# Four layers in one kernel: a running count as one scan, logits between the first expert products, constants and rounded weights in other places

## The reference

```
x = x + L0_xattn(layernorm(x), ctx);  x = x + L0_ffn(layernorm(x))
x = x + L1_xattn(...);                x = x + L1_ffn(...)   # 32 experts, 6 of 3 groups of 8, capacity 48, shared expert
x = x + L2_xattn(...);                x = x + L2_ffn(...)   # 8 experts, 2 a row, and a shared one
x = x + L3_xattn(...);                x = x + L3_ffn(...)   # 32 experts, 8 a row
```

```
# L3_ffn, t rows, 32 experts of width 96            # choice of the k largest, ties to the lower index
scores  = softmax(x @ wg.T)                         # weights, idx = top_k(scores, 8)
weights = weights / sum(weights)
out[t]  = sum over chosen e: weights[t, e] * ((silu(x @ w1[e]) * (x @ v1[e])) @ w2[e])

# L3_xattn, 16 batches of 128 rows, 16 query heads and 8 key heads of 128
xq      = fp8(bf16(clip(ln(x) / in_scale)))         # q, k, v from own rows, qx for the context
q, k    = ln(xq @ wq), ln(xq @ wk);  v = xq @ wv    # "own" pass
qx      = ln(xq @ wqx);  kx, vx = context @ w_kv_x  # "cross" pass
cat     = [softmax(q k) v, softmax(qx kx) vx]
out     = fp8(cat / smooth) @ wproj * scales
```

## Time and profile before

| | |
|---|---|
| time, median of 3 runs | 2699.9 us (2689.95 to 2700.28) |
| the profiled execution, its own time and span | 2686.2 us, 2683.2 us |
| mean granted TensorE clock | 0.923 |
| TensorE products / weight loads busy | 2252.8 us (84%) / 1647.3 us (61%) |
| VectorE, ScalarE, GpSimd busy | 1824.3 (68%), 1528.2 (57%), 1504.4 (56%) |
| layer 1's experts, 605 to 890: TensorE mostly busy | 264.1 of 295 us between 605 and 900 |
| layer 2's experts, 1110 to 1303 | TensorE 176.7 of 193 us |
| layer 3's attention, 1303 to 2236 | TensorE 850.2, VectorE 762.7, ScalarE 753.8 of 933 us |
| layer 3's experts, 2239.4 to 2683.2 | TensorE 420.7 of 444 us |

### The profile page before, as it was taken

How to read it: one execution, slowest core, us unless ns; L and a number is a source line. 1 busy time by engine, 2 the same in 40 slices (tenths; PEclk the granted TensorE clock), 3 DMA queues, 4 the chain that set the end, 5 groups by cost and what they waited for, 6 DMA issues and landing times. The chain is left out here.

```text
span 2683.2 us, 45578 instructions
## 1 busy us (share of the span) xinstructions
PE 2252.8 (84%) x14565; PEld 1647.3 (61%) x14574; DVE 1824.3 (68%) x3801; ACT 1528.2 (57%) x3413; POOL 1504.4 (56%) x1496
## 2 busy tenths in 40 slices
PE   4998243979899588699489999989999987999998
PEld 2333021537645343488367777768888876788886
DVE  3887485766446365455788888878888876566565
ACT  0777383763120166344488989878887873344443
POOL 5452103630001453386188888777888873888882
PEclk9999665898999799799799999999999998999999
DMA  5333101543040334234110000110000001433433
GB/s 131 81 91 78 56 0 61 164 131 133 4 187 8 81 82 101 69 120 125 47 33 0 0 0 0 36 38 24 4 6 4 2 1 42 116 112 113 119 111 84
DMA packets 120164, 174.19 MB, mean 65 GB/s; under 512 B 25549, under 2 KB 78957, under 8 KB 117183
## 3 DMA queue, kind: packets, MB, share of 16 engines
q1 hardware_dynamic: 119423, 171.57, 22.2%
q10 hardware_dynamic: 576, 0.52, 0.1%
HBM read 122.06 MB, written 11.48 MB: 50 GB/s over the span
## 5 line engine op out<-in xcount | busy, mean ns | idle before, releaser
L2993 POOL TENSOR_SCALAR a_raw<-a_raw,a_mu,a_dev 128x128 f32<-128x128 f32 x640 | 576.6, 913 | 10.2 <-issue 10.2
L527 DVE TENSOR_REDUCE a_mraw<-a_wave_ps 128x4 f32<-128x1024 f32 (+1 forms) x256 | 307.4, 1218 | 108.2 <-PE a_wave_ps L359 105.5
L415 ACT ACTIVATE a_et<-a_wave_ps 128x1024 f32<-128x1024 f32 x256 | 262.2, 1027 | 67.5 <-PE a_wave_ps L376 63.1
L2983 POOL TENSOR_TENSOR a_dev<-a_var,a_minus_half 128x24 f32<-128x24 f32 x32 | 135.0, 4217 | 163.1 <-DVE a_var L3351 163.1
L3189 ACT ACTIVATE a_weights<-a_sp_ps,a_nmax 128x128 f32<-128x128 f32 x512 | 184.2, 395 | 45.2 <-DVE a_nmax L3364 43.7
L1757 DVE TENSOR_TENSOR f3e_hidden_low<-f3e_hidden,f3e_hidden_high 128x512 fp32r<-128x512 f32 x96 | 117.9, 1228 | 126.1 <-ACT f3e_hidden_high L1710 125.7
L3105 PE MATMUL a_o_ps<-a_wparts,a_catq 128*128 128x256 bf16 x1536 | 188.8, 273 | 7.7 <-DVE a_catq L3385 7.6
L1618 POOL TENSOR_TENSOR f3e_product<-f3e_silu,f3e_up 128x512 f32<-128x512 f32 x96 | 143.4, 1496 | 71.5 <-PE f3e_u_ps L1637 43.5
L3022 PE MATMUL a_p_ps<-a_wkv,a_xq 128*128 128x512 f32 x640 | 179.1, 414 | 3.8 <-DVE a_wkv L3263 3.3
L393 PE MATMUL a_o_ps<-a_et,a_vt 128*32 128x256 f32 x2048 | 165.2, 395 | 17.0 <-ACT a_osb L445 15.3
L3022 PE MATMUL a_p_ps<-a_wq,a_xq 128*128 128x512 f32 x512 | 152.8, 429 | 26.9 <-ACT a_vv L3208 15.9
(11 more groups left out here) (440 smaller groups left out, 5779.3 us busy)
## 6 DMA issues: line engine op xcount, KB each, us to landing
f_w<-in_f_w SPq DMA_DIRECT2D x16, 1216.0 KB, 8.7
a_qs<-a_parts SPq DMA_DIRECT2D x144, 128.0 KB, 2.4
f_raw<-in_f_w SPq DMA_DIRECT2D x60, 256.0 KB, 3.2
a_ks<-a_parts SPq DMA_DIRECT2D x96, 128.0 KB, 2.4
f3e_spread<-f3e_shares SPq DMA_DIRECT2D x64, 192.0 KB, 3.0
f2e_spread<-f2e_shares SPq DMA_DIRECT2D x36, 256.0 KB, 3.3
f3e_spread<-f3e_shares SPq DMA_DIRECT2D x64, 128.0 KB, 3.1
f_raw<-in_f_w SPq DMA_DIRECT2D x60, 128.0 KB, 3.6
```

What stands on the lines that cost most here:

```text
L415: self.nc.scalar.activation(self.et[:, g % self.WAVES_HELD, :, :], self.wave_ps[:, self.second_place[g][0], :, :], ACT.Exp, scale=self.sca ...
L527: v.tensor_reduce(out, wave.rearrange("p u (c n) -> p u c n", n=N), AX.X, ALU.max).then_inc(self.max_taken, 1)
L2993: mm = nc.gpsimd.tensor_scalar(head, head, mu[:, parity(b), h:h + 1], dev[:, parity(b), h:h + 1], ALU.subtract, ALU.mult)
```

## The change

It has four parts.

**The running count as a scan.** `choose` makes the count with one `tensor_tensor_scan` over all rows' numbers in one line: each value is the one before times `go_on` plus `equal`. `go_on` is 1.0, and 0.0 at the first expert of each row, so that the count starts anew; `group_starts` makes it by two memsets, ahead of the router. In layer 1 the experts' and the groups' counts both go this way, and the work that stood between two steps of the old count (`between("counts")`) now comes behind the scan.

**Logits between the first gate products (layers 2 and 3).** `normalised_transposed` and `logits_and_parts` are no longer called. `run` takes their work: TensorE turns the rows in four blocks of 512, makes the logits the other way round (`make_logits`: the gate's columns are the weights, 512 rows the moving side, two products for each of four row blocks, which write to partitions 0, 32, 64 and 96), makes `gate_up(0)`, turns the logits back with four transposes (`turn_logits`), makes `gate_up(1)` and goes on. ScalarE copies the turned rows and makes the first two of the four `x_high` parts ahead of the logits, the last two behind the early evictions; `x_low` likewise, the last two behind the share copy on VectorE. SP loads the first weight tile, then the gate, then the others; GpSimd cuts the first weight tiles as they arrive. In layer 3 the choice is run inside `softmax_rows`, while ScalarE makes the exponential.

**Layer 1's constants.** `places`, `same`, `owner` and `place` are loaded at the end of SP's list in f1r, behind the experts' first six weight loads, and f1d and f1c only wait for them.

**Layer 3's attention.** The cross weights go through three raw buffers: the two halves of `wraw` and `spare`, which is the room of `exponent` and `magic`, free once the last rows are rounded (`xq_ready` of `B`). `load_cross` issues them. `next weights` has eight places: 0 to 5 in the step of batch B - 3, 6 and 7 in that of B - 2, so six tiles in the first of the two steps and two in the second, where it was four and four. `next output` 0 and 1 move to other places within their steps. The own output weights' second pair is cut inside the third step (`parts of output` and `left of output`) and not behind it. The rows of batch 1 are normalised before the low parts of the weights (`normalise_rows(1)` in `cut_weights`) and not in the task "rows" behind them. In the order lists the entries other than `next weights`, `next output` and the new two stand in the same order as before.

The core of the diff:

```diff
+def group_starts(nc, st, name, n):
+
+    go_on = st.sb(name + "_go_on", [P, B, n])
+    nc.vector.memset(go_on[:, :, :], 1.0)
+    nc.vector.drain()
+    nc.vector.memset(go_on[:, :, 0:1], 0.0)
+    nc.vector.drain()
+    return go_on
+
+
+def choose(nc, values, k, n, chosen, st, name, go_on, between=lambda place: None):
...
+    run = st.sb(name + "_run", [P, B, n])
...
     kth = over(top[:, :, k - 1], n)
+    v.tensor_tensor(equal[:, :, :], values[:, :, :], kth, ALU.is_equal)
     v.tensor_tensor(above[:, :, :], values[:, :, :], kth, ALU.is_gt)
-    v.tensor_tensor(equal[:, :, :], values[:, :, :], kth, ALU.is_equal)
     v.drain()
+    v.tensor_tensor_scan(run[:, :, :].rearrange("p b n -> p (b n)"), go_on[:, :, :].rearrange("p b n -> p (b n)"),
+                         equal[:, :, :].rearrange("p b n -> p (b n)"), 0.0, ALU.mult, ALU.add)
     v.tensor_reduce(count[:, :], above[:, :, :], AX.X, ALU.add)
-
-    src, step, turn = equal, 1, 0
-    while step < n:
-        dst = runs[turn]
-        v.tensor_tensor(dst[:, :, step:], src[:, :, step:], src[:, :, :n - step], ALU.add)
-        v.tensor_copy(dst[:, :, :step], src[:, :, :step])
-        if step == 4:
-            between("counts")
-        v.drain()
-        src, step, turn = dst, 2 * step, 1 - turn
+    between("counts")
+    v.drain()
     between("ranks")
-    v.tensor_tensor(chosen[:, :, :], src[:, :, :], over(count[:, :], n), ALU.add)
+    v.tensor_tensor(chosen[:, :, :], run[:, :, :], over(count[:, :], n), ALU.add)
...
+                    load_weights(0)
+                    sp.dma_start(gate_tile[:, :, :], gate_source).then_inc(gate_in, 16)
+                    for target, source in self.loads:
+                        sp.dma_start(target, source).then_inc(self.w_in, 16)
+                    m = 1
+                    for _ in range(self.RAW + 2 + self.early // 4):
                         load_weights(m)
                         m += 1
...
+                        pe.wait_ge(x_ready, 2 * h + j + 1)
...
+                    def turn_rows(tb):
+                        wait(pe, xs_taken, tb - 1)
+                        for u in range(4):
+                            pe.wait_ge(xs_ready, 4 * tb + u + 1)
+                            for c in range(2):
+                                last = nc.tensor.transpose(y_ps[:, tb % 2, c, u * P:u * P + P],
+                                                           xs[:, tb % 2, u, c * P:c * P + P], ident[:, :])
+                        last.then_inc(xs_turned, 1)
+
+                    def make_logits():
+                        pe.wait_ge(gate_in, 16)
+                        pe.wait_ge(xs_taken, 4)
+                        for c in range(2):
+                            for tb in range(4):
+                                last = nc.tensor.matmul(by_expert[32 * tb:32 * tb + E_GATE, :], gate_tile[:, c, :],
+                                                        xnt[:, c, tb * 512:tb * 512 + 512], start=(c == 0), stop=(c == 1))
+                        last.then_inc(logits_done, 1)
+
+                    def turn_logits():
+                        pe.wait_ge(logits_taken, 1)
+                        for k in range(4):
+                            last = nc.tensor.transpose(by_token[:, k * P:k * P + P], logits_kept[:, k * P:k * P + P],
+                                                       ident[:, :])
+                        last.then_inc(logits_turned, 1)
+
+                    for tb in range(4):
+                        turn_rows(tb)
+                    make_logits()
+                    gate_up(0)
+                    turn_logits()
+                    gate_up(1)
+                    for n in range(2, self.early):
...
+                    turned_rows(0)
+                    high_rows(0)
+                    turned_rows(1)
+                    high_rows(1)
+                    turned_rows(2)
+                    turned_rows(3)
+                    act.wait_ge(logits_done, 1)
+                    nc.scalar.copy(logits_kept, by_expert).then_inc(logits_taken, 1)
                     router_act(act)
                     for n in range(self.early):
                         evict(n)
+                    high_rows(2)
+                    high_rows(3)
...
+                    low_rows(0)
+                    low_rows(1)
+                    router_prepare()
+                    dve.wait_ge(logits_turned, 1)
+                    nc.vector.tensor_copy(logits[:, :, :].rearrange("p (t k) e -> p k t e", t=4),
+                                          by_token.rearrange("p (k t e) -> p k t e", k=4, t=4)[:, :, :, 0:E_GATE])
+                    nc.vector.drain()
                     router_dve(dve).then_inc(share_ready, 1)
                     dve.wait_ge(share_turned, B // 2)
                     nc.vector.tensor_copy(sharet[0:E, 0:T // 2], share_ps[:, 0:T // 2]).then_inc(low_copied, 1)
+                    low_rows(2)
+                    low_rows(3)
...
-            on_act, on_dve = softmax_rows(nc, block, logits, probs, E, rt, "sm")
+            on_act, on_dve = softmax_rows(nc, block, logits, probs, E, rt, "sm",
+                                           lambda dve: choose(nc, logits, K, E, chosen, rt, "ch", go_on[0]))
...
+                        sp.dma_start(places[:, :], dram["f1_places"]).then_inc(places_in, 16)
+                        sp.dma_start(same[:, :], dram["f1_same"]).then_inc(places_in, 16)
+                        sp.dma_start(owner[:, :, :].bitcast(I16), dram["f1_owner"]).then_inc(owner_in, 16)
+                        sp.dma_start(place[:, :], dram["f1_place"]).then_inc(owner_in, 16)
...
-        exponent = sb("exponent", [P, 4, 2, P], BF16)
-        magic = sb("magic", [P, 4, 2, P], BF16)
+        rounding = sb("rounding", [P, 2, 4, 2, P], BF16)
+        exponent, magic = rounding[:, 0, :, :, :], rounding[:, 1, :, :, :]
+
+        spare = rounding[:, :, :, :, :].rearrange("p e k c n -> p (e k c n)").bitcast(F32)
 
...
+                def load_cross(k):
+                    if k < 2:
+                        sp.wait_ge(out_ready, k + 3)
+                    elif k == 2:
+                        sp.wait_ge(xq_ready, B)
+                    elif k < 3 + TILES:
+                        sp.wait_ge(low_ready, TILES + k - 2)
+                    else:
+                        sp.wait_ge(out_ready, U + 1)
+                    if k < TILES:
+                        sp.dma_start(cross_staged(k), weight_piece(dram, TILES + k)).then_inc(cross_in[k % 3], 16)
+                    else:
+                        u = k - TILES
+                        sp.dma_start(out_staged(U + u), dram["a3_cross_wproj"][:, 4 * u:4 * u + 4, :]
+                                     ).then_inc(cross_in[k % 3], 16)
...
-                    if b == B - 3:
+                    if b == (B - 3 if j < 6 else B - 2):
                         if j == 0:
                             act.wait_ge(projected, L * (B - 1) + 4)
+                        if j == 4:
+                            act.wait_ge(projected, L * B)
+                        if j == 6:
+                            act.wait_ge(values_projected, M * B)
                         high_part(TILES + j)
-                    if b == B - 2:
-                        if j == 0:
-                            act.wait_ge(projected, L * B)
...
                 def cut_weights():
+                    normalise_rows(1)
                     for t in range(TILES):
                         low_part(t)
...
                 def rows_task(b, k):
-                    if not is_own(b):
-                        return
+                    if is_own(b) and not (isinstance(b, int) and b == 1):
+                        normalise_rows(b)
+
+                def normalise_rows(b):
```

235 lines of the change are left out of this document (107 added, 128 removed), and 12 rows, old and new, of tables (CROSS_ORDER, OWN_ORDER).

## The result

The changed kernel takes 2668.5 us (median of 5 runs, 2667.3 to 2673.5), the one before 2694.4 in the same comparison (5 runs, 2690.0 to 2700.3). The ratio is 0.9907, with a 95% interval of 0.9893 to 0.9921: 25 us faster, between 21 and 29. Its profiled execution has a span of 2665.4 us, where before's had 2683.2. That is only 17.8 less, because stages whose code is the same differ by some us from run to run. So each stage is measured here over several traces: of the old code there is a second trace, or a third, from the experiments that keep it, and of the changed code up to twelve, as each experiment touches few stages.

What follows compares the result with a forecast made beforehand. It took stage heads, waits for constants and layer 3's handover, not TensorE-bound loops, as the question. Terms 12.5 + 4.8 + 6.2 + 5.8 + 5.0 = 34.3 off 2686.2 gave 2651.9, 2665 in median terms; range 2646 to 2686.

Steps and rivals of the forecast that it cites:

- the handover: Layer 3's attention, four steps after the first batch: six-and-two weight tiles, third buffer, earlier output cuts gain 5.0 us.
- The worst case of the forecast: Handover: first step takes two more tiles at 2.4, second gives back only part; 3 us lost.
- the rival that had 0.18: Layer 3's attention: the handover gives its bound, 13 us and not 5, 8 more, so 2657; chance 0.18.
- layer 2's router: Layer 2's experts: router takes 8.5 us, less 0.9 for the count; in a stage term of 4.8 us.
- layer 3's experts: Largest term: new head, scan and no share wait start block 7 12.7 us earlier, 12.5 counted; bounds 9 and 14.
- The sentence on cover: Layer 3's experts: copies, DMA trips and short steps, 12.6 us, fit under five blocks, 13.7; failure costs 1 to 2.
- layer 1's constants: Layer 1's experts: loading constants in the router removes waits of 2.9 us (VectorE) and 3.3 (TensorE), together 6.2.
- the early rows: Layer 3's attention, start: second batch's rows made before the low parts, so statistics end 4.8 us earlier.
- The output pair cut inside the step: Layer 3's attention, start: cutting the second output-weight pair inside the step fills ScalarE waits, 1.0 us, between -1 and 2.
- The rival on the clock: Expert heads, layers 2 and 3: clock stays at 0.50 through early blocks, 20 us less gained, 2685; chance 0.10.
- The rival on late constants: Layer 1: constants come late behind six loads of 1.2 MB, 3 us lost, 2668; chance 0.04.
- the one on tile buffers: Layer 3's attention: tile buffers become the chain, making the kernel slower, 2714 or more; chance 0.03.

Runs made afterwards that it cites:

- the last experiment: Changed kernel with old handover places (three buffers kept), first silu and first cast early, four early blocks in layer 2: 2660.6 us, ratio 0.9862 to before.

## Why the prediction was right, and where it was not

The sign and the range held: 2668.5 in 2646 to 2686, and 0.88 had been put on faster. The single value, 2665, came nearer than its working deserves, and that is luck. The forecast gain was 34.3 us; the stages gave 22.7. What brought the two times together is the base: 2665 was reckoned from a median of 2699.9, and with five runs that median is 2694.4. The gain that was timed, 25.9 between the medians, lies at the lower edge of the 25 to 43 that got 0.60.

The step that failed most was the handover: "I take 5, ... because the second step's excess (8.6) should go mostly while the first's (6.0) grows by about 3". The direction of both was right. In eight traces the first step grew by 2.8 to 6.2, 4.2 in the mean, and the second fell by 4.6 to 6.6, 5.4 in the mean: the two together won 1.2 and not 5. Left out were the third and fourth step, which the prediction had as they were: they grew by 2.4 and by 0.9 to 3.0 us. The move of `next output` had no term of its own, and it costs 2.1 to 3.4 in the two; the rest comes with the split. The worst case of the forecast, -3, was the outcome. The reasoning from averages (no engine is full, so spreading the work must help) gave a bound of 13 that nothing came near, and with it falls the rival that had 0.18. Why the first step grows by more than the 3 us of the forecast is not shown by an experiment of its own. The trace shows the 5.2 us in which VectorE waits for a tile behind ScalarE's attention tasks.

The second was layer 2's router, taken at 8.5 us less 0.9 for the count, so 7.6. The count became one scan, but the router took 10.9. By moving it between the products it was moved beside GpSimd's products, and VectorE's steps that read two arrays then take up to 1.4 us for 0.29. Holding GpSimd showed it: 6.6. The forecast 2 us wait was 4.8, and the low clock behind it cost another 1.3. The head up to the router's start gave 4.6 (16.6 for 21.2), where only 1.7 was forecast, and 2.9 was given back behind it. So the shares were ready 27.4 us after the opening, near the forecast 27.0, by two errors that cancelled.

In layer 3's experts the steps were mostly right: router 16.3 us (16.6), scan 1.23 (1.6), no wait for the shares, wait of 2.2 before block 2 (2.1). The head was 3.3 better than forecast, mainly through the full clock in the logits (1.9 for 4.5) and in block 0 (2.9 for 4.1). The sentence on cover, that the casts, copies and trips lie "under the five blocks (13.7) before the first down product", held for the shares. It did not count GpSimd: one pair of products and one tile take it 6.2 to 8.1 us in this head, TensorE's two blocks 5.4, so while the pipeline fills TensorE runs into it. Block 7 starts 16.0 us earlier than before and the stage ends 11.2 earlier: 4.8 came back behind block 7, and the term is 11.2 and not 12.5. The 2.4 us wait and the low clock behind it are in that; how the rest of the 4.8 divides is not shown. That a faster engine meets the next one was asked for SP and the shares and not for GpSimd.

Right within 0.4 us: layer 1's constants, as pure waits in front of TensorE; and the early rows (4.7 for 4.8). The output pair cut inside the step was mis-sized, 2.2 for 1.0, just above its own bound of 2.

The rival on the clock did not come to pass in layer 3, where all seven early blocks ran at full clock. In layer 2 it came at a smaller size: the turn behind the 4.8 us wait ran at 0.54, the blocks behind it at 1.00. The rival on late constants is closed by the run with the constants alone; against the one on tile buffers stand the run with three buffers and the old places and, for six and two tiles, the trace, in which nothing waits for a load.

## What to carry to other kernels

When a step is moved under the work of another engine, list what it will run beside as well as what it no longer waits for: the same short VectorE steps cost 0.3 us each in front of GpSimd's products and up to 1.4 beside them. A pipeline that is filled faster can be held by its slowest stage while it fills (here GpSimd with 6.2 us or more for what TensorE does in 5.4), even where the loop has slack (8.2 us for the same two blocks with their down products). And a step that gets more work can lose what its neighbour gains: here moving back to the old places gave the time back, and another buffer changed nothing.

## What the runs showed of the hardware

VectorE's steps with two inputs in SBUF slow down beside GpSimd's work (1.27 for 0.29), while the reduction with one input at 1131.4 keeps its 0.25 beside a GpSimd cast. In the last experiment two such reductions lie wholly within a GpSimd product and a GpSimd subtraction and take 0.28 and 0.25. The Trainium skill ("SBUF — State Buffer", section SBUF: two separate sides) states this: VectorE operations with two such inputs and GpSimd operations that read it exclude one another for a whole instruction. The traces and the held run agree with it. Two inputs are not the only case: the copies of the old count, which have one, took up to 1.32 us in layer 3 (128x128) in the experiment with that count, where the copies of layer 2 in the kernel before, with no GpSimd work beside them, took 0.17 to 0.19.

A scan of 512 columns took 1.23 us and one of 128 took 0.42, where the passes around them take 0.69 and 0.29. That is 1.8 and 1.5 times. The rule of the Trainium skill ("DVE: opcode table, instruction layouts, handler registers and perf-mode slots", section Datapath and trigger behaviour), half throughput, shows in the difference: 384 more columns cost the scan 0.81 us and a pass 0.40.

And the same code's head in layer 2 began the router anywhere from 14.8 to 18.4 us after its opening. Its logits took 1.8 us at a granted clock of 1.00 in two of the seven traces and 3.1 to 3.5 at 0.50 to 0.57 in the others, with block 0 behind them at 2.9 to 3.9. That difference between runs of one code is larger than what most of these edits are worth; what sets the clock there from run to run is open.
